# A third place for decays, in SBUF, and another order of ScalarE's decays, in a state-space scan kernel

## The reference

```python
delta  = softplus(einsum('blr,dr->bld', d_rank, dt_proj_w) + dt_proj_b)
deltaA = exp(einsum('bld,dn->bldn', delta, A))                 # the decays
deltaB_u = einsum('bld,bln,bld->bldn', delta, Bm, x)           # the inputs
h = dA_t * h + dBu_t                                           # one step of the scan
y = einsum('bdn,bn->bd', h, C_t)
```

## Time and profile before

| | |
|---|---|
| median of 3 runs | 4593.46 us (4591.21 to 4595.19) |
| profiled execution, its own time | 4593.33 us |
| its span, first to last instruction | 4591.5 us |
| scan stage, first scan's start to last scan's start | 80.0 to 3537.3 us, 3457.3 us |
| VectorE busy in it | 3374.52 us |
| GpSimd busy in it | 3384.66 us |
| ScalarE busy in it | 2422.70 us |

### The profile page before, as it was taken

One profiled execution on the slowest core, in us unless ns is written; L12 is line 12 of the kernel. 1 busy time (PEld: TensorE's weight loads), 2 busy tenths in 40 slices (PEclk: granted clock), 3 DMA queues, 4 the chain that ended last, 5 costly groups with the idle time before them and its releaser, 6 DMA issues. The chain is left out here.

```text
span 4591.5 us, 57205 instructions
## 1 busy us (share of the span) xinstructions
PE 2737.3 (60%) x15526; PEld 1027.7 (22%) x15526; DVE 3897.8 (85%) x3322; ACT 2757.9 (60%) x4103; POOL 3507.2 (76%) x1780
## 2 busy tenths in 40 slices
PE   3556454645464645455554645464643289999997
PEld 1111111211111111111111211111211145555553
DVE  3999999999999999999999999999998645555552
ACT  5667777776767677766677777677664222222221
POOL 3999999999999999999999999999997100000000
PEclk7555565656565656555565556565655599999998
DMA  4454546363645455454545463636452300000000
GB/s 104 97 132 118 142 111 160 88 165 90 166 95 149 112 138 139 111 137 113 133 118 150 103 163 84 166 84 170 94 133 74 147 10 24 18 18 18 18 19 7
DMA packets 198208, 472.72 MB, mean 103 GB/s; under 512 B 60688, under 2 KB 61200, under 8 KB 197088
## 3 DMA queue, kind: packets, MB, share of 16 engines
q1 hardware_dynamic: 177136, 452.11, 38.8%
q0 software_dynamic: 20736, 16.88, 1.4%
HBM read 126.83 MB, written 73.43 MB: 44 GB/s over the span
## 5 line engine op out<-in xcount | busy, mean ns | idle before, releaser
L881 POOL TENSOR_TENSOR ch<-hid,cmat 128x1024 f32<-128x1024 f32 x1024 | 2388.0, 2356 | 56.9 <-DVE hid L735 39.0
L735 DVE TENSOR_TENSOR_SCAN hid<-decay,inp 128x1024 f32<-128x1024 f32 x1024 | 2291.9, 2278 | 33.4 <-ACT decay L602 32.4
L399 PE MATMUL ps_y<-ch,nsum 128*32 128x256 f32 x8192 | 998.3, 592 | 883.2 <-POOL ch L881 880.8
L602 ACT ACTIVATE decay<-delr,a_neg 128x1024 f32<-128x1024 f32 x1024 | 1138.9, 1112 | 610.0 <-DVE hid L735 593.6
L724 DVE TENSOR_TENSOR inp<-dx,bmat 128x1024 f32<-128x1024 f32 x848 | 978.2, 1215 | 63.0 <-ACT dx L610 63.0
L399 PEld LDWEIGHTS ps_y<-ch,nsum 128*32 128x32 f32 x8192 | 261.2, 146 | 1593.4 <-POOL ch L881 1346.9
L394 PE MATMUL ps_y<-xhT,dskip 128*32 128x256 f32 x2048 | 270.7, 621 | 436.0 <-DVE xr L745 436.0
L846 POOL TENSOR_TENSOR inp<-dxr,bmat 128x1024 f32<-128x1024 f32 x176 | 415.4, 2360 | 0.0
L1134 POOL DMA_INDIRECT out_rows<-row,idx_out x16 | 41.1, 2571 | 401.3 <-issue 220.2
L408 PE MATMUL ps_y<-ident,ysb 128*128 128x128 f32 x512 | 160.7, 412 | 295.2 <-ACT ysb L617 275.4
L610 ACT ACTIVATE dx<-dxr 128x1024 f32<-128x1024 f32 x256 | 259.2, 1012 | 3.0 <-DMA dxr<-dxT 3.0
(11 more groups left out here) (165 smaller groups left out, 3951.0 us busy)
## 6 DMA issues: line engine op xcount, KB each, us to landing
dxr<-dxT SPq DMA_DIRECT2D x1024, 128.0 KB, 2.4
delr<-delT SPq DMA_DIRECT2D x1024, 128.0 KB, 2.4
xr<-in_x SPq DMA_DIRECT2D x32, 1024.0 KB, 6.3
bmat<-b_and_c SPq DMA_DIRECT2D x256, 128.0 KB, 3.3
cmat<-b_and_c SPq DMA_DIRECT2D x256, 128.0 KB, 2.9
x_rows<-xr SPq DMA_DIRECT2D x16, 2048.0 KB, 7.7
out_rows<-xr SPq DMA_DIRECT2D x32, 1024.0 KB, 4.3
w<-in_w SPq DMA_DIRECT2D x2, 4096.0 KB, 23.9
```

What stands on the lines that cost most here:

```text
L399: last = pe.matmul(ps_y[q * CH:(q + 1) * CH, 0:2 * P], nsum[:], ch[:, g, q * 2 * P:(q + 1) * 2 * P], start=False, stop=(g == GROUPS - 1))
L602: nc.scalar.activation(decay[:, g % 2, :], delr[:, c % 2, :], ACT.Exp, scale=a_neg[:, i:i + 1])\
L735: nc.vector.tensor_tensor_scan(hid[:, g, :], decay[:, g % 2, :], inp[:, g, :], 0.0, ALU.mult, ALU.add).then_inc(hid_ready, 1)
L881: nc.gpsimd.tensor_tensor(ch[:, g, :], hid[:, g, :], cmat[:, g, :], ALU.mult).then_inc(ch_ready, 1)
```

## The change

A third place for decays, `decay2`, is allocated in SBUF (4 KB a partition), and the DMA scratch area is cut from 8192 to 4096 bytes a partition. Tiles 0 and 3 share `decay[:, 0]`, tile 1 has `decay[:, 1]`, tile 2 has `decay2`. ScalarE makes the decays of a chunk in the order 1, 2, 0, 3 where it made them in the order 0, 1, 2, 3. The waits follow: the decay of tile 3 waits for scan 0 of its own chunk, the other three for the scan of the same tile (tile 0: of tile 3) of the chunk before. VectorE's list is as it was, the output additions in it too; scan 2 now reads its decay from SBUF.

```diff
+DECAYS = (1, 2, 0, 3)
 YADD = 2
...
+        decay2 = sb("decay2", [P, L])
...
+        def decay_of(g):
+            return decay2[:] if g == 2 else decay[:, int(g == 1), :]
+
+        def decays(b, c, g):
+            return b * TILES + c * GROUPS + DECAYS.index(g)
...
             def exp_decay(b, c, g):
-                if has(b, 1) or c * GROUPS + g >= 2:
-                    act.wait_ge(hid_ready, tile(b, c, g) - 1)
-                if g == 0:
+                if g == 3:
+                    act.wait_ge(hid_ready, tile(b, c, 0) + 1)
+                elif has(b, 1) or c > 0:
+                    act.wait_ge(hid_ready, tile(b, c, 0) if g == 0 else tile(b, c, g) - GROUPS + 1)
+                if g == DECAYS[0]:
                     act.wait_ge(del_rep[c % 2], (b * (CHUNKS // 2) + c // 2 + 1) * 16 * NT)
                 i = c * GROUPS + g
-                nc.scalar.activation(decay[:, g % 2, :], delr[:, c % 2, :], ACT.Exp, scale=a_neg[:, i:i + 1])\
+                nc.scalar.activation(decay_of(g), delr[:, c % 2, :], ACT.Exp, scale=a_neg[:, i:i + 1])\
                     .then_inc(decay_ready, 1)
...
-                    for g in range(2):
+                    for g in DECAYS[:3]:
                         exp_decay(0, 0, g)
...
                     beside(b, par, c, 0)
-                    exp_decay(b, c, 2)
+                    exp_decay(b, c, 3)
                     if c > 0:
                         copy_y(b, c - 1)
                     elif has(b, 1):
                         copy_y(b - 1, CHUNKS - 1)
-                    exp_decay(b, c, 3)
                     if not (final and c == CHUNKS - 1):
                         copy_dx(*nxt)
+                        exp_decay(*nxt, 1)
                     beside(b, par, c, 1)
-                    for g in (0, 1):
-                        if not (final and c == CHUNKS - 1):
-                            exp_decay(*nxt, g)
-                        beside(b, par, c, 2 + g)
+                    if not (final and c == CHUNKS - 1):
+                        exp_decay(*nxt, 2)
+                    beside(b, par, c, 2)
+                    if not (final and c == CHUNKS - 1):
+                        exp_decay(*nxt, 0)
+                    beside(b, par, c, 3)
...
             def scan(b, c, g):
-                dve.wait_ge(decay_ready, tile(b, c, g) + 1)
+                dve.wait_ge(decay_ready, decays(b, c, g) + 1)
...
-                nc.vector.tensor_tensor_scan(hid[:, g, :], decay[:, g % 2, :], inp[:, g, :],
+                nc.vector.tensor_tensor_scan(hid[:, g, :], decay_of(g), inp[:, g, :],
...
-    nc = bacc.Bacc("TRN2", target_bir_lowering=False, num_devices=1, dynamic_dma_scratch_size=8192)
+    nc = bacc.Bacc("TRN2", target_bir_lowering=False, num_devices=1, dynamic_dma_scratch_size=4096)
```

## The result

The changed kernel takes **5053.61 us** (median of 4 runs, 5051.55 to 5053.72) against 4592.34 us before in the same measurement: 1.1005 times, 95% interval 1.0986 to 1.1024. It is 461 us slower; 5147 us were forecast, with a range of 4800 to 5330.

A forecast was written before the change was run, and what follows sets the result against it. GpSimd and VectorE, both within 2.4% of the 3457.3 us scan stage, bound the kernel. GpSimd's 3384.7 + 256 x 2.24 = 3958, plus 53 idle, gives 4011, 554 more: 4593 + 554 = 5147 us, range 4800 to 5330.

The forecast's parts named there:

- The term that decides: Scan stage: each scan 2, reading two SBUF inputs, holds GpSimd for its whole length, 2.24 us, 256 times; chance 0.75.
- The copies of the earlier trace: Second phase: GpSimd index copies starting inside a two-SBUF-input VectorE product ended 0.04 us behind it, seven of seven; free ones 0.18 us.
- The lower end of the prediction's own range: Scan stage: 5080 us in all, at 2.05 us a scan, if 0.18 us of a product's start runs beneath the scan.
- VectorE's own wait: Before scan 2, VectorE waits for GpSimd's running product: 0 to 2.32 us, 1.16 on average, hidden behind GpSimd.
- The upper bounds: Scan stage: 5187 us in all with the full 2.32 us VectorE wait, 5444 if half a product returns to GpSimd each time.
- Sharing: Rival at scan 2: port shared, not held, GpSimd losing at most 1.21 us a scan; middle 4770 us, chance 0.11.
- The rival of the other sign: Scan stage: scan 2 does not hold GpSimd and the new order removes decay waits; 4577 us, chance 0.10.
- that of no change: Scan stage: no hold, and the 32.4 us of decay waits come back whole elsewhere; 4593 us, chance 0.04.
- "nothing" case: Scan stage: the 32.4 us come back whole as waits for sums or at GpSimd; 4593 us, chance 0.04.
- "faster" one: Scan stage: no hold, at best 32 us of decay waits go, half likely returns at the additions; 4577 us, chance 0.10.
- The decay waits: VectorE's scans wait 32.4 us for late ScalarE decays; the new order was to bring this near nothing.
- Nothing for the scratch area: Second phase's scatters: the smaller scratch area costs 0, at most 15.6 us for a doubling of the last one.

The follow-up runs named there:

- old_order_tile2_sbuf: Kernel before, its decay order and waits kept, with tile 2's decay in SBUF and the smaller scratch area: 5055.32 us, 1.1013 times.
- new_order_psum: Changed kernel's decay order with all three places in PSUM; dx copied to SBUF unread, VectorE's inputs read tile 1's decay instead: 4587.27 us, 0.9993 times the kernel before.
- old_order_tiles13_sbuf: Kernel before, order and waits kept, with the decays of tiles 1 and 3 of each chunk in SBUF: 5556.89 us, 1.2104 times.
- input0_sbuf: Kernel before, decays unchanged, VectorE reading dx from SBUF for tile 0's input, SP waiting for that input before refilling: 4817.67 us, 1.0494 times.
- split_step: Kernel before, all decays in PSUM, last two ScalarE operations of each step size put behind tile 2's decay of the next chunk: 4590.03 us, 0.9999 times.

## Why the prediction was right, step by step

*The term that decides* was named, placed and signed rightly: scan 2 with both inputs in SBUF and GpSimd's instructions exclude each other, for whole instructions. The copies of the earlier trace rows were the right row, though one of the four was misread: the copy at 3772.17 starts not behind the product but 0.03 us before its end (3770.98 + 1.22 = 3772.20). It and one more of the trace that starts in the last 0.05 us are not held; seven that start earlier are. `old_order_tile2_sbuf` shows that the place makes the loss without the new order, `new_order_psum` that without the place there is none, `old_order_tiles13_sbuf` that it goes with the number of scans, and `input0_sbuf` that it goes with the length of VectorE's instruction.

*Its size was too large.* 2.24 us a scan were taken, 504.7 / 256 = 1.97 us are measured. The lower end of the prediction's own range had a price of 2.05 us, since the start of GpSimd's product may run beneath the scan, with the free copy's 0.18 us as the measure. It does, and the scan's own start runs beneath the product before it: of the scan's 2.26 us 0.29 do not count (2.26 - 1.97), about 0.2 for the one (a product takes 2.35 us and ends 2.15 behind the scan) and about 0.1 for the other (the scan ends 2.15 us behind the product). 256 x 0.27 is 69 of the 97 us by which the stage was missed (4011 forecast, 3914 measured). The other 28 are GpSimd's idle time, forecast at 53 us and measured at 24.8: once it is the bound it hardly ever waits for a scan.

*VectorE's own wait*, which no row of before showed, was taken as 1.16 us on average and as hidden. Scans are busy 2482.8 us where they were 2291.9, so it is 0.75 us a scan, and it is hidden: VectorE idles 340 us of the stage beside it (3914.1 - 3573.9). The upper bounds were not needed.

*The rivals.* Sharing is out: the held product ends 2.15 us behind the scan, which is nearly all of its 2.35; only some 0.2 us of it lay beneath the scan. The rival of the other sign, and that of no change, fell with it. What they said of the order by itself could be tried: in `split_step` the decay waits are removed, and come back as waits for sums, which is the "nothing" case rather than the 16 us of the "faster" one.

*The decay waits* were to fall to near nothing. They are 27.1 us, none of them at tile 2: 18 of the 19 waits are at tile 0, 15 of these in chunk 14, as here:

```profile
1027.66 7.49 DVE L749 TENSOR_TENSOR_SCAN hid<-decay,inp 128x1024 f32<-128x1024 f32 x3 [1.34 <-ACT decay L614]
```

Tile 0's decay, now the third of the chunk, stands there behind the next step size's `te`, before which ScalarE is idle for 4.65 us. That step was wrong for this kernel. It seems to have cost nothing, since VectorE waits for GpSimd anyway: `old_order_tile2_sbuf` has 88.0 us of decay waits and takes the same time within 2 us. With the places in PSUM the same order leaves 1.5 us, and `te` starts after 0.43 us of idle there; so the order fell short only beside the held engines. What delays `te` was not tested.

*Nothing for the scratch area* is right: the second phase is the same to 0.1 us, with half the area. *The rule of the Trainium skill* ("SBUF — State Buffer", "Who interferes with whom") is that whoever issues first has the shared pair of ports for the whole instruction, and the other is blocked. The runs agree but for the starts of the instructions, the 0.29 us above.

## What to carry to other kernels

Before a buffer is moved from PSUM to SBUF, ask which VectorE instruction reads it and whether its other input is in SBUF too; if GpSimd reads SBUF at that time, each such instruction costs GpSimd nearly its whole length (here 1.97 us of a scan's 2.26, 0.97 of a product's 1.21), and VectorE waits for GpSimd's running one. Copies into PSUM that look needless (here `dx`) may be there to keep one of the two inputs out of SBUF: reading `dx` from SBUF for one tile a chunk cost 227 us. And where two engines are both at 98% of a stage, a wait removed on one may come back at what is late next: here 27 us of decay waits became 24 us of waits for sums.

## What the runs showed of the hardware beyond that

The two engines took turns. Wherever scan 2 came while a GpSimd product was in work, it ended 2.15 to 2.18 us behind that product's end (5th to 95th percentile of 255 scans in the changed kernel), ahead of the next product, although GpSimd had that one ready each time. The one exception, the longest scan with 4.53 us, began 0.08 us before a product's end and ended 2.15 us behind the next product: it came too late by its own start. A scan alone takes 2.26 us, so about 0.1 us of it runs beneath the product.

A short GpSimd instruction was held as a long one: the 128x8 instructions of `input0_sbuf` waited, as the copies of one element in the second phase did, until the end of VectorE's instruction (1.19 us for 0.2).
